# Local attention: ScalarE seeds the score banks with the mask, VectorE rotates before it sums squares, ScalarE begins a step with the exponentials

## The reference

```python
def local_attention(q, k, v):              # 16 heads of 64, windows of 32
    bk2, bv2 = look(bk), look(bv)          # this window and the one before it: 64 keys
    mask = (it < jb) | (it > jb + w) | (jb == -1)
    sim = jnp.einsum('bhwie,bhwje->bhwij', bq, bk2) * QK_SCALE
    sim = jnp.where(mask, -jnp.finfo(sim.dtype).max, sim)
    return softmax(sim, -1) @ bv2

def attn_layer(x, Wqkv, qs, ksc, Wo):
    q, k, v = split(x @ Wqkv)              # 3 x 1024 columns
    q, k = l2norm(q) * qs, l2norm(k) * ksc # sums of squares over 64
    q = q * cos * scale + rotate_half(q) * sin * scale     # k likewise
    return local_attention(q, k, v) @ Wo

for i in range(6):
    x = attn_layer(shift_tokens(x), ...) + x
    x = ffn_layer(shift_tokens(x), ...) + x    # layer norm, gated by an exact gelu
```

## Time and profile before

| what | value |
|---|---|
| three runs | 5451.67 us median, 5448.25 to 5453.95 |
| profiled execution | 5438.05 us, its span 5436.3 us |
| busy share of the span | TensorE 87%, VectorE 76%, ScalarE 62%, GpSimd 50% |
| mean granted clock | 0.94 |
| the two stacks | about 535 to 2230 us, and 3675 to 5415 us |

### The profile page before, as it was taken

The page is one execution under the profiler, slowest core; times in us unless marked ns, Lnnn a source line. Parts: engine busy times, 40 slices in busy tenths (PEclk is TensorE's granted clock), DMA queues, the critical chain, the costliest instruction groups (busy, mean ns, idle before and its releaser), DMA issues. The chain is left out here.

```text
span 5436.3 us, 135547 instructions
## 1 busy us (share of the span) xinstructions
PE 4737.4 (87%) x51446; PEld 3032.6 (56%) x51638; DVE 4133.6 (76%) x8982; ACT 3352.3 (62%) x7201; POOL 2735.3 (50%) x3646
## 2 busy tenths in 40 slices
PE   4775899999999999777777778658999999999997
PEld 2232566666666666434444344335666666666665
DVE  5897677777777777479898999966777777777774
ACT  2432677777777777444545444435777777777775
POOL 1221666666666666223233333316666666666663
PEclk7898999999999999988888889869999999999999
DMA  0000222222222222100000000002222223222221
GB/s 18 0 0 12 75 71 71 68 69 69 78 62 74 67 76 63 27 15 2 2 2 2 1 2 2 2 1 79 67 73 65 77 62 79 65 74 67 76 63 40
DMA packets 162491, 247.18 MB, mean 45 GB/s; under 512 B 36228, under 2 KB 56640, under 8 KB 161734
## 3 DMA queue, kind: packets, MB, share of 16 engines
q1 hardware_dynamic: 161862, 238.65, 16.9%
HBM read 36.15 MB, written 1.05 MB: 7 GB/s over the span
## 5 line engine op out<-in xcount | busy, mean ns | idle before, releaser
L940 POOL TENSOR_TENSOR f_rope<-f_rope,f_t 128x1024 f32<-128x1024 f32 x384 | 905.7, 2359 | 524.2 <-DVE f_t L854 524.2
L953 POOL TENSOR_TENSOR f_rope<-f_rope,f_rn 128x1024 f32<-128x1024 f32 x384 | 730.6, 1903 | 56.7 <-POOL f_rn L932 2.6
L490 PE MATMUL psum<-f_wqkv,f_xs 128*128 128x512 f32 x1536 | 729.6, 598 | 22.6 <-DVE f_t L854 22.6
L859 DVE TENSOR_REDUCE f_ss<-f_sq 128x16 f32<-128x1024 f32 x384 | 459.9, 1198 | 335.9 <-ACT f_sq L721 333.0
L1827 POOL TENSOR_SCALAR tk_scores<-tk_scores,tk_m 128x408 f32<-128x408 f32 (+28 forms) x232 | 239.2, 1031 | 783.2 <-DVE tk_m L1787 619.3
L684 ACT ACTIVATE f_kT<-psum 64x512 f32<-64x512 f32 (+1 forms) x960 | 485.3, 525 | 83.4 <-PE psum L481 73.8
L721 ACT ACTIVATE f_sq<-psum 128x1024 f32<-128x1024 f32 x384 | 393.3, 1024 | 218.7 <-PE psum L490 218.3
L854 DVE TENSOR_TENSOR f_t<-psum,f_rot 128x1024 f32<-128x1024 f32 x384 | 466.0, 1213 | 0.0
L850 DVE TENSOR_TENSOR f_rope<-psum,f_rot 128x1024 f32<-128x1024 f32 x384 | 465.3, 1212 | 0.0
L876 DVE TENSOR_REDUCE f_den<-f_prob 128x16 f32<-128x1024 f32 x192 | 234.2, 1220 | 296.0 <-ACT f_prob L726 296.0
L490 PEld LDWEIGHTS psum<-f_wqkv,f_xs 128*128 128x128 f32 x1536 | 279.3, 192 | 305.9 <-issue 298.7
(11 more groups left out here) (240 smaller groups left out, 9759.7 us busy)
## 6 DMA issues: line engine op xcount, KB each, us to landing
f_v<-f_v_tok SPq DMA_DIRECT2D x1152, 128.0 KB, 2.4
f_v<-f_v_tok SPq DMA_DIRECT2D x768, 64.0 KB, 2.0
f_wqkv<-in_Wqkv SPq DMA_DIRECT2D x36, 512.0 KB, 4.0
f_wo<-in_Wo SPq DMA_DIRECT2D x12, 512.0 KB, 4.0
f_w<-in_W SPq DMA_DIRECT2D x12, 341.0 KB, 3.3
f_w<-in_W SPq DMA_DIRECT2D x24, 64.0 KB
tk_wkv<-in_Wkv SPq DMA_DIRECT2D x1, 1024.0 KB
out<-y_tok SPq DMA_DIRECT2D x4, 256.0 KB, 2.5
```

Source lines behind the costliest of these rows:

```text
L490: last = pe.matmul(psum[:, n, :], xs[:, j % 2, :], wqkv[:, INNER * which + 512 * n:INNER * which + 512 * (n + 1)], start=True, stop=True)
L859: dve.tensor_reduce(ss[:, H * half:H * (half + 1)], sq[:, half, :, :], AX_X, ALU.add).then_inc(s[f"{name}_ss"], 1)
L940: pool.tensor_tensor(part, part, t2[:, half, :, :], ALU.add).then_inc(s[f"{name}_added"], 1)
L953: pool.tensor_tensor(part, part, rn[:, H * half:H * (half + 1)].unsqueeze(2).to_broadcast([P, H, DH]), ALU.mult).then_inc(s[f"{name}_norme ...
```

## The change

It has three parts. First, the mask no longer goes into the score banks by two matmuls. ScalarE copies it there from `band`, after the copies to `qT` and after the scaled output has been read out of those banks (`on_done`), and tells TensorE by a new semaphore, `seeded`. So that the scores are added to it, the matmuls that weigh the values set their start flag for one column block in four. The first steps of a stack, which have nothing to weigh, keep the matmuls. Second, VectorE rotates keys and queries before it sums their squares, the sum of the queries' squares goes behind the difference at the end of a step, and GpSimd clamps after it has added. Third, ScalarE starts a step with the exponentials and one value copy, and takes the query inverse after them.

```diff
 # TensorE, weigh()
-    probT[...], v2[...], start=True, stop=True)
+    probT[...], v2[...], start=(c % 4 == 0), stop=True, skip_group_check=True)
 # TensorE, score()
     if on(g, 2):
-        wait(pe, "on_done", through(g, 2))
-    for half in range(2):
+        wait(pe, "seeded", g - 1)
+    for half in range(0 if on(g, 2) else 2):
         pe.matmul(psum[:, 4 + half, :], k.ident_bf[:, :], k.band[...], start=True, stop=False, ...)
 # ScalarE, start of a step
+    exponent()
+    evacuate(0 if j == 2 else 1)
     if on(g, 1):
         inverse("q", 0, through(g, 1))
-    evacuate(0 if j == 2 else 1)
-    exponent()
     square(1, "k")
 # ScalarE, after the copies to qT
+    if on(g, 1) and on(g, 2):
+        wait(act, "on_done", through(g, 2))
+        mask = k.band[:, int((j - 1) % 4 == 0), 0:1, :].to_broadcast([P, H, 2 * WIN])
+        copy(sc_bank, mask).then_inc(s["seeded"], 1)
 # VectorE
-    sum_squares(g, 1, "k")
     rotate(g, j, 1, "k")
+    sum_squares(g, 1, "k")
 ...
-    sum_squares(g, 0, "q")
     rotate(g, j, 0, "q")
     (maximum and difference of the scores)
+    sum_squares(g, 0, "q")
 # GpSimd
     norm(0, "q", g - 1, (j - 1) % 2)
-    clamp(1, "k")
     add(1, "k")
+    clamp(1, "k")
     norm(1, "k", g, j % 2)
-    clamp(0, "q")
     (residual)
     add(0, "q")
+    clamp(0, "q")
```

More of the change, by code:

```diff
@@ L335, in ffn_stack @@
                   "qt0_full", "qt1_full", "qt0_evac", "qt1_evac", "ot0_full", "ot1_full", "ot0_evac", "ot1_evac",
-                  "scores", "top", "sub_done", "exp_done", "summed", "rden_done", "pv_done", "on_done", "wo_full", "wo_evac", "res_done",
+                  "seeded", "scores", "top", "sub_done", "exp_done", "summed", "rden_done", "pv_done", "on_done", "wo_full", "wo_evac", "res_done",
                   "ff_in", "ff_mean", "ff_centred", "ff_squared", "ff_var", "ff_x", "ff_logged", "ff_y", "ff_polish", "ff_rstd", "ff_wide", "ff_scaled",
@@ L604, in weigh @@
                                     last = pe.matmul(psum[WIN * w:WIN * (w + 1), 4 + c // 4, (c % 4) * P:(c % 4 + 1) * P],
-                                                     probT[:, c, WIN * w:WIN * (w + 1)], v2[:, j % 2, w, :, c, :], start=True, stop=True)
+                                                     probT[:, c, WIN * w:WIN * (w + 1)], v2[:, j % 2, w, :, c, :],
+                                                     start=(c % 4 == 0), stop=True, skip_group_check=True)
                             last.then_inc(s["pv_done"], 1)
@@ L626, in score @@
                                 wait(pe, f"qt{n}_evac", through(g, 1))
+                            sj = (j - 1) % 4
                             if on(g, 2):
-                                wait(pe, "on_done", through(g, 2))
-                            sj = (j - 1) % 4
-                            for half in range(2):
+                                wait(pe, "seeded", g - 1)
+                            for half in range(0 if on(g, 2) else 2):
                                 pe.matmul(psum[:, 4 + half, :], k.ident_bf[:, :], k.band[:, int(sj == 0), :, :].rearrange("p h w -> p (h w)"),
@@ L881, in step @@
                             tables(L)
+                        rotate(g, j, 1, "k")
                         sum_squares(g, 1, "k")
-                        rotate(g, j, 1, "k")
                     if f is not None and j == 0:
@@ L914, in step @@
                         dve.tensor_tensor(prob[:, :, :], sc_bank, top[:, :].unsqueeze(2).to_broadcast([P, H, 2 * WIN]), ALU.subtract).then_inc(s["sub_done"], 1)
+                    if on(g, 0):
+                        sum_squares(g, 0, "q")
                 def group(L, b, g, ff):
@@ L962, in step @@
                     if on(g, 0):
+                        add(1, "k")
                         clamp(1, "k")
-                        add(1, "k")
                         norm(1, "k", g, j % 2)
-                        clamp(0, "q")
                     if on(g, 3):
```

## The result

The changed program takes **5553.71 us** (median of four runs, 5551.09 to 5557.08) against 5451.05 for the kernel before, run beside it: a ratio of 1.0189, 95% interval 1.0171 to 1.0206. That is 103 us slower. The profiled execution took 5555.06 us. One run of a kernel of the experiments, the one with three swaps (5822.86 us, granted clock 0.80 against about 0.94 elsewhere) was in a slow state, and no ratio counts it.

What follows compares the result with a forecast made beforehand. Bound taken: dependency loops, after the change the ScalarE, VectorE and GpSimd chain. Groups 1.93 us slower, 44 times 85 us, plus 1 for short groups: 5438.05 to 5524 profiled, plus 13.6 gives 5537 us; range 5490 to 5600.

Steps and rivals of the forecast that it cites:

- A: Start of a step's key squares on ScalarE; key clamp predicted to end 6.08 us later, key inverse to start at 6.11.
- Z: Start of a step's query squares on ScalarE, predicted 8.51 us after A, with the next A 7.75 after it.
- The four steps: Steps from A to A, predicted 16.26 us for j = 3, 16.79 for j = 0, 17.18 for j = 1, 22.03 for j = 2.
- the group: Four steps with a feed-forward, from A to A: predicted 72.26 us against 70.33 before, 1.93 slower.
- GpSimd's queue: GpSimd's in-order work delays the key add in j = 1 by 0.92 us and the end of j = 2 by 1.24.
- the key inverse's wait in j = 1: Predicted sign on ScalarE: the key inverse waits for GpSimd over 2 us in j = 1.
- 44 groups: 85 us: Predicted loss over the two stacks' 44 groups with a feed-forward, at 1.93 us each.
- The old loop: Rival, chance 0.12: the loop through TensorE still decides, only shorter, 2.6 us a group faster, 5336 us.
- No change: Rival, chance 0.05: GpSimd's queue does not bite in j = 1 and at the end of j = 2; 5442 us.
- The clock: Rival, chance 0.04: TensorE gets holes and one step in ten runs at 1.2 GHz; 5806 us.
- The seed was not dear: Rival, chance 0.03: ScalarE's mask copy takes twice its price, 0.95 us more in four steps of 46 groups; 5712 us.
- The sum by busy time: Reading rejected by the prediction: TensorE 99% busy, over a microsecond off its queue, 6% off each step.

Runs made afterwards that it cites:

- the one with three swaps: Changed kernel; key clamp before key add; in j = 2 query clamp before query add and VectorE's value scaling before the second gate: 5394.67 us, 0.9897.
- the query clamp: Changed kernel with GpSimd's query clamp moved, in j = 2 alone, ahead of the residual and the query add: 5579.22 us, 1.0248 of the kernel before.

## Why the prediction was right, and where it was short

**The mechanism.** A step lasts as long as the longer of two loops, the one through TensorE and the chain of ScalarE, VectorE and GpSimd. The steps without feed-forward show it cleanly:

| kernel | mask matmuls | key clamp behind add | seed | step |
|---|---|---|---|---|
| before | yes | no | no | 16.01 |
| seed alone | no | no | yes | 15.56 |
| reorders without seed | yes | yes | no | 16.00 |
| change, key clamp put back | no | no | yes | 15.57 |
| the change | no | yes | yes | 16.28 |

TensorE's loop is 16.0 with the mask matmuls and 15.56 without: at either value two kernels agree that differ in the order of the other engines. The chain is 16.28 with wait and seed. Without the seed's 0.95 it would be about 15.3 (an estimate, 16.28 less 0.95), under TensorE's 16.0, and so hidden. The seed alone costs 0.2%, the reorders (second and third part) without it 0.3%, both together 1.9%: what each adds to the chain fits into its slack, and the sum does not. This is the prediction's point in the earlier trace rows, where 1.40 us of slack stood against an add of 2.36.

**The terms.** The clamp ended at A + 6.18 (said 6.08), the inverse began 0.03 behind it (0.03), the seed held ScalarE 0.95 (0.93), Z came at A + 8.61 (8.51) and the next A 7.67 later (7.75). The four steps are within 0.16 of those predicted, the group within 0.02. That so little is left is luck in part: j = 1 came out 0.12 longer and j = 2 0.16 shorter, and Z is 0.10 late where the rest is 0.08 short. GpSimd's queue did bite: the add of j = 1 started at A + 4.50 (said 4.40), and the end of j = 2 waited for the clamp, 1.10 us. One sign missed: the key inverse's wait in j = 1 is 1.59 us, not over 2. ScalarE was not there at A + 4.84 as the prediction had it, because its copies to kT had themselves waited 0.76 us for TensorE's transposes.

**Where it fell short** is the sum's "44 groups: 85 us". It took the first step of a layer for an ordinary one. The change left the tables where they stood, but brought the key rotation, and with it the chain, directly behind them, and one product there met GpSimd's scaling: 1.71 us more than its usual 0.28. That is 17 us that the prediction doesn't have, 1.67 in each of ten steps, and with it nearly all of the 16.7 between 5537 and 5553.7. Moving the tables took 21 us away, and the one layer start without the meeting was 1.92 us shorter than the other nine; together they show it.

**The rivals.** The old loop did not stay: the wait is in the trace, and it takes the key clamp's old place to make the loop through TensorE decide again (15.56). "No change" fell with the waits of j = 1 and j = 2, which the trace has. The clock stayed at 0.99 to 1.00 in the stack. The seed was not dear. The sum by busy time, 6% off each step, did not come either: the seed alone, without the mask matmuls, takes 0.45 us (3%) off a step without feed-forward and nothing off a group (70.32). So far the rule of the Trainium skill ("Trainium Kernel Development and Optimization", Performance Expectations) that matmul busy time is a bad metric is borne out.

**What my expectations got wrong.** Four of them took a step from one kernel and set it beside the steps of another: the query clamp, the seed alone, the reorders alone and the combination. With the query clamp and in the combination, time taken out of j = 2 came back in j = 3, where an earlier A met GpSimd's held-up queue or TensorE's output passes of the feed-forward. With the seed alone and the reorders alone I had j = 3 too short, 17.2 and 15.8 where 17.55 and 17.52 were measured. The second part alone and the third alone were dearer than said, in part for waits that I had not counted: the first step of a layer, and the clamp that stands idle for the late sum of squares. A group has to be followed as a whole, from A to A of the next group.

About 15 us of the profiled executions' difference (5555.06 against 5438.05) belong to the stretch between the stacks, from the last A of one to the first of the other, which took 1474 to 1492 us in the kernels here without any edit there. Its cause was not looked for. The medians lie 103 us apart, about what the two stacks differ by in the profiled executions (105 us).

## What to carry to other kernels

Where engines run in order and are joined by semaphores, write down the time of each loop of dependencies, not the engine's load, and give each wait its slack: two edits that each fit into the slack can cost 2% together. When a small instruction that another engine waits for is moved behind a large one, it inherits the large one's length, and moved ahead, it holds the large one up until its own input is there: here exchanging a key clamp of 0.24 us and an add of 2.36 was worth 2.4% of the time, and the like exchange for the queries in j = 2 cost 0.6%. And look at the rare step, here the first of a layer, with its own rows: what the common step's order hides may stand bare in it.

## What the runs showed of the hardware

I had not expected a product of 128x128 on VectorE to last about seven times its usual length. In all ten layer starts of the changed kernel that follow another layer, one product of `rot_base` and `qk_gain`, usually 0.28 us long, took 1.99 to 2.00 us and ended 0.15 behind the end of GpSimd's scaling of `rope`, which had started 0.06 before it (1107.28 and 1107.34 in the rows of the layer's start). With the seed alone, the first product of the tables (128x256, usually 0.42 us) began 0.25 to 0.63 us before the scaling's end; it took 0.53 to 0.91 us and ended 0.28 us behind the scaling in all ten layer starts. So in these runs the product ended a fixed time behind the scaling, however much of the scaling was left. VectorE's rotation multiplies, which read one operand out of PSUM, took 1.21 to 1.23 us with or without a large GpSimd operation beside them. The Trainium skill ("SBUF — State Buffer", Who interferes with whom) says that a VectorE instruction with two inputs in SBUF contends with a GpSimd instruction that reads SBUF. In its section "SBUF: two separate sides" it says that whichever of the two starts first gets the shared ports for its whole instruction, and the other blocks. The trace agrees (1.99 us beside the scaling of 1.90, 0.50 a pair ahead of it). No run here tells the ports from another cause of this wait.

A ScalarE copy of 128x1024 into PSUM took 1.03 us, against 1.02 for the squares out of PSUM and 1.06 for the exponentials in place: no difference that a step could use.
